# Strassen's scheme on twelve instead of eight chunks per block, with the half chunk, the folds and two layer-0 products laid out anew

## The chip, the core and the metric

The kernel runs on one core of a Trainium2 chip. The metric is the device time of one execution in microseconds (us). The engines are called PE (TensorE, matrix products), DVE (VectorE, elementwise work), ACT (ScalarE), POOL (GpSimd, which here only issues transfers that add) and SP (SyncE, which issues the loads).

## The reference

Three layers of a compressed interaction network. For each of 2048 batch items, with x of 39 fields by 16 channels and `prev` = x at first:

```python
for i, f in enumerate(CIN_LAYERS):              # f = 128 in each of the three layers
    h = prev.shape[1]                           # 39, then 64, then 64
    Wr = Ws[i].reshape(h, M, f)                 # M = 39
    z = relu(einsum('bhk,bmk,hmf->bfk', prev, x0, Wr) + bs[i][None, :, None])
    results.append(z[:, :64]); prev = z[:, 64:]
pooled = jnp.sum(jnp.concatenate(results, axis=1), axis=-1)
y = pooled @ W_lin
```

Everything is float32.

## The kernel before

**Blocks.** A block is 64 batch items by 16 channels, so 1024 columns (`NB`), treated as two halves of 512 (`BANK`, one bank of PSUM). There are 32 blocks. Blocks 0, 1, 30 and 31 are written out; blocks 2 to 29 run in a loop of 14 turns with two blocks each, an even one (`u` = 0) and an odd one (`u` = 1). In each turn of the loop DVE, PE, ACT, POOL and SP run their own instruction streams and meet at semaphores.

**Products.** In layers 1 and 2 the sum over pairs (h, m) is cut into 20 chunks of 128 pairs. DVE multiplies rows of `prev` with rows of x that were loaded repeated over partitions (`x_bc`), L408 for two chunks at once (128x2048) and L414 for one (128x1024), into a ring `prod` of 8 slots; PE multiplies a slot with the chunk's weights. `prod_ready` tells PE that a chunk is there, `chunk_used` tells DVE that a slot is free. The last field makes a half chunk, called T1: 64 rows for each half of the columns (two instructions of 64x512 in layer 1, L412; one of 64x1024 in layer 2, L405, into `left2`). Layer 0 has 6 chunks of its own (L381), made for the block that follows, and a remainder of 28 rows (`product_left`, once in a turn). PE works with two column halves of its array side by side: matmuls of 64 output rows.

**Order on PE in a looped block:** layer 1, layer 0 of the next block (L722), layer 2 (L921, L928). Layer 1 has 20 positions. Positions 0 to 15 are done for both halves of the columns, then positions 16 to 19 for the first half (`half_full` then lets ACT start with it), then 16 to 19 for the second half.

**Strassen's scheme.** On the second half of the columns, four pairs of chunks in layer 1 (`PAIR_TILES`, two pairs for each of the two layouts `a` of `prev`) go through seven quarter products of 256 columns (L850) instead of eight. It needs sums on DVE: `diff` (L474) and `more` (L479), made after each group of four chunks. Part of the quarter products collects in `acc0`. ACT copies one part out (L1090), DVE combines the parts in five small additions (L507 to L514) and adds them to `acc1` (L517, `mix`). That last addition waits until PE has consumed position 15, and PE waits for it (`mix_added`) before the second halves of positions 16 to 19. One field of each pair of x tiles must have another added to it, which POOL does by a transfer with addition (`add_tile`, L671).

**Evacuation and channel sums.** ACT applies bias and relu and spreads the state over partitions (`evacuate1_by_half`, `evacuate0`): `prev_ready` lets DVE begin the next layer. The kept halves (`res01`, `res2`) are folded twice by transfers with addition (`fold`, L677 and L680) and then reduced on DVE over the rest (L537) and weighed into `pool` (L549, L563).

Of the kernel before, what the change touches and what calls it, by code (L numbers as in the profile page):

```python
# [14 lines left out]
def cin_kernel(nc, x, w0, w0_mirror, w1, w2, b0, b1, b2, w_lin, out, dims):  # L15
# [29 lines left out]
    RUN_OF = [n for n, (_, w) in enumerate(RUNS) for _ in range(w)]  # L45
    NR = len(RUNS)
# [15 lines left out]
    MIX = 5  # L62
    assert NH == 2 and 2 * CH % RING == 0 and NBLK % U == 0 and HALF == 2 * QUAD and M == QPT * T + 3
# [8 lines left out]
    BC_LOADS = [QPT] * len(XB_GROUPS) + [1, 2]  # L72
# [20 lines left out]
    assert sorted(ORDER_PAIRED) == list(range(CH)) and all(p % RING + FOUR <= RING for p in FOUR_AT)  # L93

    with ExitStack() as ctx:
# [24 lines left out]
        x_rep_s = sb("x_rep_s", [P, BANK])  # L120
# [17 lines left out]
        sum01 = sb("sum01", [P, BB])  # L138
        sum2 = sb("sum2", [P, BB])
        pool = sb("pool", [P, BATCH])  # L140
        left2 = sb("left2", [P, NB])
# [1086 lines left out]
```

## Time and profile before

| | |
|---|---|
| median of 3 runs | 1970.98 us (1970.87 to 1971.71) |
| the profiled execution | 1970.57 us, its span 1968.6 us |
| PE busy | 1962.8 us (100%) |
| DVE busy | 1912.1 us (97%) |
| ACT busy | 586.7 us (30%) |
| POOL busy | 154.5 us (8%) |
| moved by transfers | 327.45 MB, mean 166 GB/s |
| granted TensorE clock | 1.000 |

Busy is the time in which at least one instruction of the engine is under way. Matmuls overlap in the pipeline, so PE's share says that it had work, not how fast that work went. The idle time before an instruction is put down to what ended it last.

### The profile page before, as it was taken

What the parts mean: (1) busy time and instruction counts of PE and PEld (TensorE: products, weight loads), DVE (VectorE), ACT (ScalarE), POOL (GpSimd) and SP (SyncE); (2) the same over time, 40 slices, a digit from 0 to 9 for tenths busy, and PEclk for the clock granted to TensorE, in tenths of its full rate; (3) what the DMA queues carried; (4) which work ended last, traced back from release to release, by engine and by line L of the source; (5) the groups of instructions that cost most, each with busy time, mean ns of one, the idle gap of its engine ahead of it and who ended that gap; (6) DMA issues with size and microseconds to landing.
All of it is one profiled execution on the core that took longest, in us unless ns stands there. A gap on an engine that the chain in (4) does not pass through costs nothing.

```text
span 1968.6 us, 29931 instructions
## 1 busy us (share of the span) xinstructions
PE 1962.8 (100%) x10304; PEld 739.1 (38%) x10304; DVE 1912.1 (97%) x1445; ACT 586.7 (30%) x717; POOL 154.5 (8%) x186
## 2 busy tenths in 40 slices
PE   9999999999999999999999999999999999999999
PEld 3333343333333333333343333333333333333333
DVE  8989999999999999999999999999999999999988
ACT  2333223332133322333222332223332133322332
POOL 1001000010100100001000010010100100000000
DMA  7999988788977889778798777987778977789720
GB/s 179 189 194 186 188 174 169 162 171 175 191 165 158 175 167 199 168 154 175 159 207 169 154 173 162 195 183 157 168 159 183 192 160 166 164 175 197 149 43 1
DMA packets 122523, 327.45 MB, mean 166 GB/s; under 512 B 24529, under 2 KB 43370, under 8 KB 122501
## 3 DMA queue, kind: packets, MB, share of 16 engines
q1 hardware_dynamic: 97539, 303.05, 71.2%
q0 software_dynamic: 24192, 23.87, 7.8%
q10 hardware_dynamic: 770, 0.23, 0.1%
q8 instruction: 15, 0.25, 0.1%
q14 instruction: 7, 0.06, 0.0%
HBM read 303.11 MB, written 0.01 MB: 154 GB/s over the span
## 4 chain that ended last, share of the span: by engine, by line
PE 97%; DVE 2%; DMA 0%; issue 0%; ACT 0%; ACTq 0%; DVEq 0%
PE acc L845 37%; PE acc L722 23%; PE acc L921 20%; PE acc L850 11%; PE acc L910 2%; PE acc L714 2%; DVE prod L408 1%; PE acc L789 1%; PE acc L935 1%; PE acc L928 1%; DMA bias<-b 0%; DVE prod L414 0%; PE acc L729 0%; ACT prev L1043 0%; ACTq L1141 0%
## 5 line engine op out<-in xcount | busy, mean ns | idle before, releaser
L408 DVE TENSOR_TENSOR prod<-prev,x_bc 128x2048 f32<-128x2048 f32 x511 | 1139.7, 2283 | 11.1 <-PE acc L722 9.4
L845 PE MATMUL acc<-prod,w_sb 128*64 128x512 f32 x3360 | 748.4, 593 | 0.0
L921 PE MATMUL acc<-prod,w_sb 128*64 128x512 f32 x1064 | 462.4, 593 | 0.1
L845 PEld LDWEIGHTS acc<-prod,w_sb 128*64 128x64 f32 x3360 | 237.3, 137 | 442.4 <-issue 391.4
L928 PE MATMUL acc<-prod,w_sb 128*64 128x512 f32 x840 | 384.3, 593 | 0.0
L722 PE MATMUL acc<-x_rot,w_sb 128*64 128x512 f32 x1240 | 277.5, 593 | 0.0
L1090 ACT ACTIVATE diff<-acc 64x256 f32<-64x256 f32 x56 | 21.3, 380 | 735.3 <-PE acc L850 735.0
L921 PEld LDWEIGHTS acc<-prod,w_sb 128*64 128x64 f32 x1064 | 143.9, 137 | 248.3 <-issue 193.5
L414 DVE TENSOR_TENSOR prod<-prev,x_bc 128x1024 f32<-128x1024 f32 x193 | 230.0, 1218 | 1.5
L381 DVE TENSOR_TENSOR x_rot<-x_rot,x_rep 128x1024 f32<-128x1024 f32 (+1 forms) x186 | 214.5, 1222 | 1.3 <-issue 0.3
L1014 ACT ACTIVATE prev<-acc,bias 32x1024 f32<-32x1024 f32 x140 | 155.1, 1108 | 3.1 <-DVE prod L408 0.9
L722 PEld LDWEIGHTS acc<-x_rot,w_sb 128*64 128x64 f32 x1240 | 87.8, 137 | 179.9 <-issue 164.8
L1107 ACT ACTIVATE prev<-acc,bias 32x512 f32<-32x512 f32 x224 | 152.4, 680 | 3.2
L1005 ACT ACTIVATE prev<-acc,bias 64x1024 f32<-64x1024 f32 x68 | 75.5, 1111 | 250.3 <-PE acc L722 221.7
L850 PE MATMUL acc<-prod,w_sb 128*64 128x256 f32 x672 | 134.0, 379 | 0.0
L722 PE MATMUL acc<-prod,w_sb 128*64 128x512 f32 x600 | 130.1, 593 | 0.6 <-DVE prod L408 0.5
L1101 ACT ACTIVATE prev<-acc,bias 64x512 f32<-64x512 f32 x112 | 76.5, 683 | 171.7 <-PE acc L845 170.7
L928 PEld LDWEIGHTS acc<-prod,w_sb 128*64 128x64 f32 x840 | 113.5, 137 | 8.8
L850 PEld LDWEIGHTS acc<-prod,w_sb 128*64 128x64 f32 x672 | 62.8, 137 | 64.0 <-issue 64.0
L671 POOL DMA_DIRECT2D x_bc<-x_bc x56 | 48.8, 872 | 411.9 <-DMA x_bc<-x 315.5
L677 POOL DMA_DIRECT2D res<-res x42 | 36.5, 869 | 559.7 <-ACT res L1126 363.2
L722 PEld LDWEIGHTS acc<-prod,w_sb 128*64 128x64 f32 x600 | 44.2, 137 | 86.1 <-issue 82.4
(100 smaller groups left out, 1246.7 us busy)
## 6 DMA issues: line engine op xcount, KB each, us to landing
x_bc<-x SPq DMA_DIRECT2D x312, 256.0 KB, 15.5
x_bc<-x SPq DMA_DIRECT2D x156, 512.0 KB, 21.4
x_rot<-x SPq DMA_DIRECT2D x155, 312.0 KB
x_rot<-x SPq DMA_DIRECT2D x217, 156.0 KB
x_bc<-x SPq DMA_DIRECT2D x124, 128.0 KB, 11.0
x_rep<-x SPq DMA_DIRECT2D x62, 192.0 KB
x_bc<-x_bc POOLq DMA_DIRECT2D x56, 128.0 KB, 10.1
x_rot<-x SPq DMA_DIRECT2D x124, 44.0 KB
```

Of the source, the lines that this page charges most:

```text
L381: nc.vector.tensor_tensor(x_rot[0:rows, c, :], rot, x_rep[0:rows, :], ALU.mult).then_inc(prod0_ready, 1)
L408: mul = nc.vector.tensor_tensor(prod[:, s:s + w, :], twice, x_bc[:, u, t:t + w, :], ALU.mult)
L414: mul = nc.vector.tensor_tensor(prod[:, s, :], old[:], new, ALU.mult)
L722: mm = nc.tensor.matmul(acc[f, h, :], w[:, f], rhs[:, BANK * h:BANK * h + BANK], start=start, stop=stop)
L845: mm = nc.tensor.matmul(acc1[f, h, :], w[:, f], prod[:, s, BANK * h:BANK * h + BANK], start=False, stop=stop, skip_group_check=closed)
L850: return nc.tensor.matmul(acc, w, rhs, start=start, stop=stop, skip_group_check=True)
L921: nc.tensor.matmul(acc2[0:HALF, u, :], w, prod[:, s, 0:BANK], start=(pos == 1), stop=False)
L928: mm = nc.tensor.matmul(acc2[HALF:P, u, :], w, prod[:, s, BANK:NB], start=(pos == 1), stop=False)
L1005: op = nc.scalar.activation(dst[0][HALF * g:HALF * g + HALF, :], src, ACT.Relu, bias=bias[HALF:P, layer:layer + 1])
L1014: op = nc.scalar.activation(dst[1][QUAD * q:QUAD * q + QUAD, :], acc[h:h + QUAD, :, :].rearrange("p h n -> p (h n)"), ACT.Relu, bias=bias[ ...
L1101: op = nc.scalar.activation(prev[1][0][HALF * g:HALF * g + HALF, cols], acc1[HALF:P, h, :], ACT.Relu, bias=bias[HALF:P, 1:2])
L1107: op = nc.scalar.activation(prev[1][1][QUAD * q:QUAD * q + QUAD, cols], acc1[f:f + QUAD, h, :], ACT.Relu, bias=bias[f:f + QUAD, 1:2])
```

## The change

The change has five parts. (1) `PAIR_TILES` gets a third pair: six chunks instead of four stand together in `prod` for each `a` (`six_chunks`), `diff` grows from 128x512 to 128x768 and `more` from 128x1024 to 128x1536 elements, and the third pair's `diff` product is done as two matmuls of 128 columns. Now positions 0 to 16 are consumed whole (`BY_HALF` = 17) and 17 to 19 by halves. (2) T1 is one DVE instruction of 128x512 in both layers, from `prev_t1`, which ACT writes with two more activations of 64x512 (`spread_t1`), and `x_t1`, which is loaded at half the size; in layer 2 it comes fifth. (3) In layer 2 the ring has a ninth slot, which shares its memory with `more`; SP's loads for `product_left` wait until `more` has been used, since `x_rep_s` lies there too, and `product_left` moves into the even block's layer 2. (4) `res01` is folded four times and `res2` three times, the folds of both alternating on POOL's queue with the tile additions of the next block (`block_adds`); DVE no longer reduces in the loop, it only weighs the folded columns, after the fifth run of layer 2. (5) Two of the six layer-0 products come ahead of `mix`, whose first addition waits for the first of ACT's two copies only.

```diff
+    T1_AT = 4
+    RUNS2 = [*RUNS[1:T1_AT + 1], RUNS[0], *RUNS[T1_AT + 1:]]
+    RUN_OF2 = [next(n for n, (p, w) in enumerate(RUNS2) if p <= pos < p + w) for pos in range(CH)]
...
-    PAIR_TILES = [(1, 2), (3, 4)]
-    FOUR = 2 * len(PAIR_TILES)
-    FOUR_AT = 2, 10
-    ORDER_PAIRED = [CH - 1, 0, *range(1, 1 + FOUR), *range(1 + FOUR, T), *range(T + 2, T + 2 + FOUR), T, T + 1,
-                    *range(T + 2 + FOUR, CH - 1)]
-    RUNS_PAIRED = [(0, 1), (1, 1), *((p, 2) for p in range(2, 14, 2)), (14, 1), (15, 1), (16, 2), (18, 2)]
+    PAIR_TILES = [(1, 2), (3, 4), (5, 6)]
+    SIX = 2 * len(PAIR_TILES)
+    SIX_AT = 2, 10
+    ORDER_PAIRED = [CH - 1, 0, *range(1, 1 + SIX), *range(1 + SIX, T), *range(T + 2, T + 2 + SIX), T, T + 1,
+                    *range(T + 2 + SIX, CH - 1)]
+    RUNS_PAIRED = [(0, 1), (1, 1), *((p, 2) for p in range(2, 16, 2)), (16, 1), (17, 1), (18, 2)]
     RUN_OF_PAIRED = [n for n, (_, w) in enumerate(RUNS_PAIRED) for _ in range(w)]
-    BY_HALF = 16
+    BY_HALF = 17
     MIX = 5
+    RING2 = RING + 1
+    SLOT2 = [(pos - 2) % RING2 for pos in range(CH)]
...
-        x_bc = sb("x_bc", [P, U, T + 2, NB])
+        x_bc = sb("x_bc", [P, U, T + 1, NB])
+        x_t1 = sb("x_t1", [P, U, BANK])
         prev = [[sb(f"prev{l}{a}", [P, NB]) for a in range(2)] for l in (1, 2)]
-        prod = sb("prod", [P, RING, NB])
-
-        diff = sb("diff", [P, 2, QTR])
-        more = sb("more", [P, 2, 2, QTR])
-        mixed = diff
+        prev_t1 = sb("prev_t1", [P, BANK])
+        prod_all = sb("prod", [P, RING * NB + len(PAIR_TILES) * BANK])
+        prod = prod_all[:, 0:(RING + 1) * NB].rearrange("p (s n) -> p s n", n=NB)
+
+        diff = sb("diff", [P, len(PAIR_TILES), QTR])
+        more = prod_all[:, RING * NB:].rearrange("p (k n c) -> p k n c", n=2, c=QTR)
+        x_rep_s = more[:, len(PAIR_TILES) - 1, :, :].rearrange("p n c -> p (n c)")
+        sum01, sum2 = diff[:, 0, 0:BB], diff[:, 0, BB:2 * BB]
+        mixed = diff[:, 0:2, :]
...
+                        sp.wait_ge(more_used, i * 2 - 1)
+                        sp.sem_inc(pairs_asked, 1)
...
-                if layer == 2 and t == T1:
-                    k = slice(HALF * u, HALF * u + HALF)
-                    mul = nc.vector.tensor_tensor(left2[k, :], old[k, :], new[k, :], ALU.mult)
+                s = (phase + pos) % RING if slots is None else slots[pos]
+                old = prev[layer - 1][a]
+                if t == T1:
+                    to = left2[:, u, :] if layer == 2 else prod[:, s, 0:BANK]
+                    mul = nc.vector.tensor_tensor(to, prev_t1[:], x_t1[:, u, :], ALU.mult)
                 elif w == 2:
                     twice = old[:].rearrange("p (o n) -> p o n", o=1).to_broadcast([P, w, NB])
                     mul = nc.vector.tensor_tensor(prod[:, s:s + w, :], twice, x_bc[:, u, t:t + w, :], ALU.mult)
-                elif t == T1:
-                    for h in range(NH):
-                        k, cols = slice(HALF * h, HALF * h + HALF), slice(BANK * h, BANK * h + BANK)
-                        mul = nc.vector.tensor_tensor(prod[k, s, cols], old[k, cols], new[k, cols], ALU.mult)
                 else:
-                    mul = nc.vector.tensor_tensor(prod[:, s, :], old[:], new, ALU.mult)
+                    mul = nc.vector.tensor_tensor(prod[:, s, :], old[:], x_bc[:, u, t, :], ALU.mult)
...
+                    elif pos in (0, 1, 11):
+                        dve.wait_ge(prev_ready[1], i * 2 + (1 if pos == 1 else 2))
                     if pos > 0:
-                        dve.wait_ge(chunk_used, first + pos + w)
-                    product(2, n, u, phase, runs=runs)
+                        dve.wait_ge(chunk_used, first + (pos + w - (1 if slots is SLOT2 else 0)))
...
+            def weigh_folded01(i, a, folded):
+
+                dve.wait_ge(folded01, folded)
+                nc.vector.tensor_scalar(pool[:, bass.ds(i * BB, BB)], res01[a][:, 0:BB], wl_col[:, 0:1], None,
+                                        ALU.mult).then_inc(pooled01, 1)
...
                     products1_paired(i, u, j + u, j, i * (2 * CH))
+                    products0(i + 1, range(2))
                     mix(i, u)
-                    if u == U - 1:
-                        product_left(j * U + (1 + U))
-                    channel_sum2(i - 2, folded=i * 32 - 32)
-                    products0(i + 1)
-                    channel_sum01(i - 1, 1 - u, folded=i * 32 - 32)
-                    products2(i, u, i * (2 * CH) + CH)
+                    products0(i + 1, range(2, C0))
+                    products2(i, u, i * (2 * CH) + CH, range(5))
+                    weigh_folded01(i - 1, 1 - u, i * (16 * FOLDS01) - 16 * FOLDS01)
+                    weigh_folded2(i - 2, i * (16 * FOLDS2) - 16 * FOLDS2)
+                    if u == 0:
+                        products2(i, u, i * (2 * CH) + CH, range(5, TAIL_RUNS))
+                        product_left(i + (1 + U))
+                        products2(i, u, i * (2 * CH) + CH, range(TAIL_RUNS, NR))
+                    else:
+                        products2(i, u, i * (2 * CH) + CH, range(5, NR))
...
+            def block_adds(i, u, loaded=None):
+
+                done01, done2 = i * (16 * FOLDS01) - 32 * FOLDS01, i * (16 * FOLDS2) - 32 * FOLDS2
+                pool.wait_ge(res01_ready, i * 2 + 1)
+                pool.wait_ge(pooled01, i)
+                fold(res01[1 - u], NB, 0, folded01, done01)
+                fold(res01[1 - u], NB, 1, folded01, done01)
+                pool.wait_ge(res2_ready, i + 1)
+                fold(res2, BANK, 0, folded2, done2)
+                fold(res01[1 - u], NB, 2, folded01, done01)
+                fold(res2, BANK, 1, folded2, done2)
+                if loaded is not None:
+                    add_tile(1 - u, 0, loaded)
+                fold(res01[1 - u], NB, 3, folded01, done01)
+                fold(res2, BANK, 2, folded2, done2)
+                if loaded is not None:
+                    for n in range(1, len(PAIR_TILES)):
+                        add_tile(1 - u, n, loaded)
...
-                quarter(acc0[low, u, 0, q2], s6[1], diff[:, 1, :], stop=(a == 1))
-                quarter(acc0[up, u, 0, q2], s6[0], diff[:, 0, :], stop=(a == 1)).then_inc(more_used, 1)
+                quarter(acc0[low, u, 0, q2], s6[1], diff[:, 1, :])
+                quarter(acc0[up, u, 0, q2], s6[0], diff[:, 0, :])
+                half = QTR // 2
+                quarter(acc0[low, u, 0, BANK - QTR:BANK - half], s6[2], diff[:, 2, 0:half], stop=(a == 1))
+                quarter(acc0[up, u, 0, BANK - half:BANK], s6[2], diff[:, 2, half:QTR], stop=(a == 1)).then_inc(more_used, 1)
...
+            def spread_t1(h, acc, layer, u):
+                k = slice(HALF * (h ^ u), HALF * (h ^ u) + HALF)
+                return nc.scalar.activation(prev_t1[k, :], acc[HALF:P, h, :], ACT.Relu,
+                                            bias=bias[HALF:P, layer:layer + 1])
...
-                    for q in range(QPT):
-                        f = HALF + QUAD * ((q + 1) % 2)
-                        op = nc.scalar.activation(prev[1][1][QUAD * q:QUAD * q + QUAD, cols], acc1[f:f + QUAD, h, :],
-                                                  ACT.Relu, bias=bias[f:f + QUAD, 1:2])
-                op.then_inc(prev_ready[1], 1)
+                    spread_t1(h, acc1, 1, a)
+                spread_turned(prev[1], acc1, 1)```

DVE at the end of a looped block's layer 1. Before, the products of positions 18 and 19 are followed at once by `mix`:

```order
L495 REGISTER_ALU
L408 TENSOR_TENSOR prod<-prev,x_bc 128x2048
L506 REGISTER_ALU
L507 TENSOR_TENSOR diff<-acc,diff 64x256
L508 ISA
L509 TENSOR_TENSOR diff<-acc,diff 64x256
L510 REGISTER_ALU
L511 TENSOR_TENSOR diff<-acc,diff 64x256
L512 TENSOR_TENSOR diff<-acc,diff 64x256
```

DVE at the same place in the changed kernel (L424 is the product of two chunks, L395 a layer-0 product):

```order
L509 REGISTER_ALU
L424 TENSOR_TENSOR prod<-prev,x_bc 128x2048
L405 ISA
L409 REGISTER_ALU
L395 TENSOR_TENSOR x_rot<-x_rot,x_rep 128x1024 x2
L521 TENSOR_TENSOR diff<-acc,diff 64x256
L522 ISA
L524 TENSOR_TENSOR diff<-acc,diff 64x256
```

Two of the six layer-0 products have moved from behind `mix` to a place ahead of it.

DVE between layer 0 and layer 2 before, with the reduction of `res01`'s folded columns and T1 as the first product of layer 2:

```order
L381 TENSOR_TENSOR x_rot<-x_rot,x_rep 128x1024
L381 TENSOR_TENSOR x_rot<-x_rot,x_rep 117x1024
L537 TENSOR_REDUCE sum<-x_seed 128x64
L548 REGISTER_ALU
L549 ISA
L549 TENSOR_SCALAR pool<-sum,wl_col 128x64
L405 TENSOR_TENSOR left<-prev,x_bc 64x1024
L532 REGISTER_ALU
L414 TENSOR_TENSOR prod<-prev,x_bc 128x1024
```

The changed kernel's DVE in layer 2 of an even block, from the run of positions 6 and 7 on:

```order
L424 TENSOR_TENSOR prod<-prev,x_bc 128x2048
L421 TENSOR_TENSOR left<-prev_t,x_t 128x512
L564 ISA
L565 ISA
L565 TENSOR_SCALAR pool<-x_seed,wl_col 128x64
L570 ISA
L573 ISA
L573 SCALAR_TENSOR_TENSOR pool<-res,wl_col,pool 128x64
L545 REGISTER_ALU
L424 TENSOR_TENSOR prod<-prev,x_bc 128x2048
```

The reductions are gone, T1 has half the columns, and T1 and both weighings stand behind four runs of layer 2.

PE behind a group of Strassen pairs before:

```order
L870 REGISTER_ALU
L850 MATMUL acc<-more,w_sums 64x256
L850 MATMUL acc<-more,w_sb 64x256
L850 MATMUL acc<-more,w_sums 64x256
L850 MATMUL acc<-more,w_sb 64x256
L850 MATMUL acc<-diff,w_sums 64x256 x2
```

PE at the same place in the changed kernel:

```order
L909 REGISTER_ALU
L889 MATMUL acc<-more,w_sums 64x256
L889 MATMUL acc<-more,w_sb 64x256
L889 MATMUL acc<-more,w_sums 64x256
L889 MATMUL acc<-more,w_sb 64x256
L889 MATMUL acc<-more,w_sums 64x256
L889 MATMUL acc<-more,w_sb 64x256
L889 MATMUL acc<-diff,w_sums 64x256 x2
L889 MATMUL acc<-diff,w_sums 64x128 x2
```

One pair's `more` products and two matmuls of 128 columns are added; ahead of them the third pair has taken the place of two chunks that were done whole.

## Rows read from the trace of the kernel before

**Rows 1.** The page: shares of the chain that ended last, by engine.
```profile
PE 97%; DVE 2%; DMA 0%; issue 0%; ACT 0%; ACTq 0%; DVEq 0%
```

**Rows 2.** Waits: engine, line, waited for: us in total, times, longest us.
```profile
PEld acc L921 <- DVE prod L408: 34.0, 83, 1.0
...
PEld acc L845 <- DVE prod L408: 25.6, 69, 0.8
...
DVE acc L517 <- PE acc L845: 5.1, 14, 0.4
```

**Rows 3.** Windows: the blocks 15 (odd) and 16 (even), from 938.25 us on.
```profile
938.25:1000.14 61.89, 61.89 (x334) 23.60 (x336) 61.14 (x48) 17.80 (x22) 4.35 (x5) 1.00 0.82 172
1000.14:1059.74 59.60, 59.60 (x321) 22.98 (x313) 58.46 (x45) 19.07 (x24) 6.08 (x7) 1.00 0.82 174
```

**Rows 4.** Timeline of PE in block 16: start us, us, engine, line, operation.
```profile
1000.14 1.04 PE L714 MATMUL acc<-prod,w_sb 64*64 64x512 f32 x8
...
1022.22 0.60 PE L850 MATMUL acc<-diff,w_sums 128*64 128x256 f32 x4
1022.65 10.47 PE L845 MATMUL acc<-prod,w_sb 128*64 128x512 f32 x48
1032.95 0.60 PE L722 MATMUL acc<-x_rot,w_sb 128*64 128x512 f32 x2
```

**Rows 5.** Timeline of DVE, from block 16's addition to block 17's.
```profile
1026.31 0.70 DVE L517 TENSOR_TENSOR acc<-acc,diff 128x512 f32<-128x512 f32 x1 [0.38 <-PE acc L845]
1027.04 0.29 DVE L537 TENSOR_REDUCE sum<-res 128x64 f32<-128x128 f32 x1
1027.49 0.28 DVE L563 SCALAR_TENSOR_TENSOR pool<-sum,wl_col,pool 128x64 f32 x1 [0.17 <-DVE sum L537]
1027.85 6.90 DVE L381 TENSOR_TENSOR x_rot<-x_rot,x_rep 128x1024 f32<-128x1024 f32 x6
1034.67 0.60 DVE L537 TENSOR_REDUCE sum<-x_seed 128x64 f32<-128x256 f32 x1
...
1035.59 1.21 DVE L405 TENSOR_TENSOR left<-prev,x_bc 64x1024 f32<-64x1024 f32 x1
...
1057.74 1.38 DVE L412 TENSOR_TENSOR prod<-prev,x_bc 64x512 f32<-64x512 f32 x2
...
1086.63 0.70 DVE L517 TENSOR_TENSOR acc<-acc,diff 128x512 f32<-128x512 f32 x1
```

**Rows 6.** Groups of like instructions: busy us, mean ns of one.
```profile
L479 DVE TENSOR_TENSOR more<-prod,diff 128x1024 f32<-128x1024 f32 x56 | 68.6, 1225 | 1.9
...
L474 DVE TENSOR_TENSOR diff<-prod 128x512 f32<-128x512 f32 x56 | 38.7, 692 | 1.9
...
L850 PEld LDWEIGHTS acc<-more,w_sums 128*64 128x64 f32 x224 | 30.7, 137 | 16.2
...
L995 PE MATMUL acc<-res,wl_all 128*32 128x64 f32 x16 | 1.1, 218 | 0.0
```

**Rows 7.** Timeline of ACT in block 16.
```profile
1022.87 0.77 ACT L1090 ACTIVATE diff<-acc 64x256 f32<-64x256 f32 x2 [21.71 <-PE acc L850]
...
1033.90 1.38 ACT L1101 ACTIVATE prev<-acc,bias 64x512 f32<-64x512 f32 x2
```

**Rows 8.** Timeline of POOL: folds and tile additions that it issues.
```profile
880.30 0.87 POOL L677 DMA_DIRECT2D res<-res  x1 [18.74 <-ACT res L1126]
892.61 0.86 POOL L680 DMA_DIRECT2D res<-res  x1 [11.44 <-DMA res<-res]
...
956.42 0.86 POOL L671 DMA_DIRECT2D x_bc<-x_bc  x1 [12.87 <-DMA x_bc<-x]
961.40 0.86 POOL L671 DMA_DIRECT2D x_bc<-x_bc  x1 [4.12 <-DMA x_bc<-x]
```

**Rows 9.** Timeline of ACT and DVE in the last block.
```profile
1937.13 2.25 ACT L1117 ACTIVATE prev<-acc,bias 64x1024 f32<-64x1024 f32 x2 [33.94 <-PE acc L722]
...
1940.31 1.22 DVE L405 TENSOR_TENSOR left<-prev,x_bc 64x1024 f32<-64x1024 f32 x1
```

More of the change, by code:

```diff
@@ L92, in cin_kernel @@
     assert RUN_OF[TAIL] == TAIL_RUNS and all((CH + TAIL + p) % RING + w <= RING for p, w in RUNS_LAST)
-    assert sorted(ORDER_PAIRED) == list(range(CH)) and all(p % RING + FOUR <= RING for p in FOUR_AT)
+    assert sorted(ORDER_PAIRED) == list(range(CH)) and all(p % RING + SIX <= RING for p in SIX_AT)
     with ExitStack() as ctx:
@@ L516, in mix, with products2 @@
                 dve.wait_ge(chunk_used, i * (2 * CH) + (RING + BY_HALF))
-                nc.vector.tensor_tensor(acc1[:, 1, :], acc1[:, 1, :], mixed[:].rearrange("p n c -> p (n c)"),
+                nc.vector.tensor_tensor(acc1[:, 1, :], acc1[:, 1, :], mixed.rearrange("p n c -> p (n c)"),
                                         ALU.add).then_inc(mix_added, 1)
-            def products2(i, u, first, part=range(NR), last=False, phase=CH):
-                runs = RUNS_END if last else RUNS
+            def products2(i, u, first, part=range(NR), last=False, slots=SLOT2):
+                runs = RUNS_END if last else RUNS2
                 for n in part:
@@ L695, in _ @@
             nc.gpsimd.tensor_tensor(w2_diff[:], second, first, ALU.subtract).then_inc(w2_diff_ready, 1)
-            with pool.Fori(1, STEPS - 1) as j:
-                for u in range(U):
-                    i = j * U + u
-                    for n in range(len(PAIR_TILES)):
-                        add_tile(u, n, (j + u) * (16 * QPT))
-                    pool.wait_ge(res01_ready, i * 2 + 1)
-                    fold(res01[1 - u], NB, folded01, i * 32 - 64)
-                    pool.wait_ge(res2_ready, i + 1)
-                    fold(res2, BANK, folded2, i * 32 - 64)
+            def block_adds(i, u, loaded=None):
[15 more added lines that the diff above has]
+                        add_tile(1 - u, n, loaded)
@@ L706, in _, with split @@
+            for n in range(len(PAIR_TILES)):
+                add_tile(0, n, 16 * QPT)
+            with pool.Fori(1, STEPS - 2) as j:
+                for u in range(U):
+                    block_adds(j * U + u, u, j * (16 * QPT) + 16 * QPT)
+            block_adds(LAST - 3, 0, (STEPS - 1) * (16 * QPT))
+            block_adds(LAST - 2, 1)
         @block.tensor
         def _(pe):
-            def split(acc, w, rhs, start, stop):
+            def split(acc, w, s, u, start, stop):
                 for h in range(NH):
-                    k = slice(HALF * h, HALF * h + HALF)
+                    k = slice(HALF * (h ^ u), HALF * (h ^ u) + HALF)
@@ L887, in layer1_paired @@
                     c = ORDER_PAIRED[pos]
-                    if pos in FOUR_AT:
-                        four_chunks(i, u, FOUR_AT.index(pos), runs)
-                    elif not any(p < pos < p + FOUR for p in FOUR_AT):
+                    if pos in SIX_AT:
+                        six_chunks(i, u, SIX_AT.index(pos), runs)
+                    elif not any(p < pos < p + SIX for p in SIX_AT):
                         pe.wait_ge(prod_ready, runs + RUN_OF_PAIRED[pos] + 1)
@@ L902, in layer1_paired, with layer2 @@
                     layer0_left(range(U), ahead)
-            def layer2(i, u, runs, part=range(1, CH), opened=False, run_of=RUN_OF, phase=CH):
+            def layer2(i, u, runs, part=range(1, CH), opened=False, run_of=RUN_OF2, slots=SLOT2):
                 if part[0] == 1 and not opened:
@@ L954, in _ @@
             layer2(0, 0, NR)
[L955 removed]
+            layer1(1, 1, 2 * NR, ahead=PAIR0 + 1)
             layer0(0, PAIR0 + 2)
@@ L1006, in spread @@
                                               bias=bias[HALF:P, layer:layer + 1])
-                op.then_inc(prev_ready[layer], 1)
+                if layer == 1:
+                    op.then_inc(prev_ready[layer], 1)
+                if t1_free is not None:
+                    act.wait_ge(prod_ready, t1_free)
+                for h in range(NH):
+                    op = spread_t1(h, acc, layer, u)
+                if layer == 0:
+                    op.then_inc(prev_ready[layer], 1)
                 spread_turned(dst, acc, layer)
```

217 lines of the change are left out of this document (109 added, 108 removed).

## The prediction, made before the changed kernel was run

> **What bounds the kernel now.** I read the page first. The chain that ended last lies on PE for 97% [rows 1], and PE and DVE are both busy almost throughout, so neither name alone is an answer. Busy says little of PE, so I looked at its pace: 48 matmuls of 512 columns start within 1032.95 - 1022.65 = 10.30 us, 0.215 us each, and four of 256 columns take 1022.65 - 1022.22 = 0.43 us, 0.108 us each [rows 4]. Time goes with the columns; there is no fixed part to see and hardly a gap.
>
> The loop is very regular. One turn is 61.89 us for the odd and 59.60 us for the even block, 121.49 us; DVE is busy for 61.14 + 58.46 = 119.60 us of it [rows 3]. Its missing 1.9 us are mostly the short gaps between instructions that depend on each other. The only real wait on PE is at L517 in the even block, 0.38 us, once in each of the 14 turns [rows 2, 5]. PE in turn waits for products of DVE, often and for at most 1.0 us, and those are waits of weight loads, most of which the running matmuls cover [rows 2]. I let 0.15 us a turn of them reach the matmuls; that is a choice, since no row separates them.
>
> So the limit is a loop through both engines: from the even block's L517 DVE works without a real pause to the odd block's L517 (1086.63 - 1026.31 = 60.32 us [rows 5]), and from there PE works without one to the next even block. Shortening one engine alone gives nothing; both get work removed here, and DVE gets some added. The question is which of the two hand-overs is late afterwards.
>
> **PE, own work.** A Strassen pair saves one quarter product, two matmuls of 256 columns in one of two column halves: 0.215 us by [rows 4]. Two pairs more per block, four per turn: -0.86 us a turn. The two matmuls of 128 columns in `six_chunks` count as one quarter. Nothing before has that shape; matmuls of 64 columns take 1.1 us for 16 [rows 6], 0.07 us each, so 128 columns are between 0.054 (by columns) and 0.14 us (twice that). As two column halves work side by side I take the columns' share; the upper bound would add at most 4 x 0.17 = 0.7 us a turn.
>
> **The weight loads** are what speaks against finer cutting. The change has 20 matmuls, and so 20 weight loads, more per block: 8 behind each of the two groups, 4 in layer 2. A load is 137 ns long [rows 6]. The steady 0.215 us per matmul, each with a load of its own, and the unchanged pace at 256 columns [rows 4] say that they are covered. I take nothing.
> The Trainium skill, page "TensorE: Matmul & The Clock Gate", section "The mechanism", says that a weight load overlaps with running matmuls only where the row group differs. All these matmuls use all 128 rows. By its section "LDWEIGHTS (loading the stationary operand)" 64 columns load in 53 ns, which makes an estimate of 20 x 53 ns = 1.1 us per block, 30 us in 28 blocks, and 1993 us in place of the sum below. The trace does not bear it out: at 0.215 us per matmul there is no room for uncovered loads [rows 4].
>
> **DVE, own work**, between the even block's L517 and the odd one's, where it decides:
> - the two reductions and their gaps and weighings go: 1027.85 - 1027.04 = 0.81 us, and 1035.59 - 1034.67 = 0.92 us [rows 5];
> - T1 in layer 2, 1.21 us long [rows 5], becomes 128x512, 0.69 us by `diff`'s shape [rows 6]: -0.52 us. T1 in layer 1, two pieces in 1.38 us [rows 5], becomes one: -0.69 us;
> - `diff` and `more` grow by 256 and 512 elements. A layer-0 product costs 6.90 / 6 = 1.15 us for 1024 [rows 5] and `diff` 0.69 us for 512, `more` 1.225 us for 1024 [rows 6], so about 1.04 ns per element: 0.80 us for a group, +1.60 us for two;
> - the two weighings remain, 0.25 to 0.3 us each and a gap: +0.6 us (0.4 if their register work is covered);
> - `product_left` moves into this stretch from behind the odd L517. It has `diff`'s old shape, 0.69 us, of which independent instructions overlap some 0.08 (1.21 long, 1.15 apart is the same effect): +0.6 us.
>
> Sum: 60.32 - 0.81 - 0.92 - 0.52 - 0.69 + 1.60 + 0.6 + 0.6 = 60.2 us. Over a whole turn DVE loses work: -1.73 x 2 - 1.21 x 2 + 3.2 + 1.2 = -1.5 us.
>
> **ACT.** The copies of L1090 start 0.04 us behind the `diff` matmuls' end and take 0.77 us for two [rows 7]; as the first addition now needs one only, `mix` starts 0.38 us earlier against PE. For layer 2 DVE needs PE's last second half, 0.17 us of pipeline, and then 1.38 us of two activations (as at 1033.90 [rows 7]). Before, the four turned copies of the first half came in between; now one T1 copy does, and ACT is ready in time. PE's second halves end at 29.81 + 2.58 = 32.4 us from the block's start (below), so the state is ready at 34.0; DVE gets there at 28.4 + 0.73 + 4 x 1.15 = 33.7. It waits 0.3 us where it waited for nothing: the stretch becomes 60.5 us. The extra T1 activations (4 x 0.68 us per block) lie in ACT's 70% idle time.
>
> **The hand-overs.** Times from a block's start on PE (1000.14 before [rows 4]). Position 14 begins at 22.5 and 16 at 25.94 before; with two pairs more, 16 begins at 25.5. It takes 8 x 0.215 = 1.72, the first halves of 17 to 19 take 2.58, so the second halves begin at 29.8 and layer 0 at 32.4 (32.81 before [rows 4], less 0.43).
> Even block: `more_used` comes at 25.7 with the pipeline's 0.17, the first copy ends at 26.1; DVE is there already, so it idles. The five additions take 2.3 us, L517 starts at 28.4 and ends at 29.1. PE needs it at 29.8: in time by 0.7 us.
> Odd block: DVE arrives 60.5 us later, at 88.9, ends L517 at 89.6 and PE hears of it at 89.65. PE's second halves could begin at (59.60 - 0.43) + 29.8 = 89.0. **PE waits 0.6 us, where it did not wait before.** This is the two-ahead order's price: the two layer-0 products fill DVE's idle time in the even block and delay `mix` by 2.3 us in the odd one. Cover before was 4 first halves, 3.4 us; now it is 3, 2.6 us. With DVE's figures 0.2 us lower the wait is 0.4; I take 0.5 us (0 to 1.2).
> Layer 2 itself gets easier: DVE makes its first product 34.0 - 32.4 = 1.6 us behind PE's start of layer 0, before 1035.59 + 1.13 - 1032.95 = 3.8 us [rows 4, 5], so the 0.15 us of waits at its end go.
>
> **Sum.** A turn: -0.86 - 0.15 + 0.5 = -0.51 us; 14 turns: -7.1 us. Blocks 0, 1, 30, 31 have no Strassen; in the last block DVE runs without a pause from 1940.31 and T1 there is 0.52 us shorter, while ACT, from 1937.13, then needs 1.38 us for T1 before the 2.2 us of state [rows 9], 1940.8 us: in time. -0.5 us. Together -7.6 us on the profiled 1970.57 us, 1963.0 us. The median of the runs is 0.4 us above the profiled one: **1963.3 us**. About 0.2% (4 us) is what a measurement of this kernel can tell from no change.
>
> **The folds**, if they are covered, cost nothing; the cover is thin in one place. `res2` of an even turn is issued at 880.30, and the step behind it goes out at 892.61 once that has landed [rows 8]: 12.3 us a step while the bulk loads run. Three steps end at 917.2. DVE asks in block 14 (which began at 1000.14 - 121.49 = 878.65) at 28.4 + 5.6 + four runs (7 chunks of 1.1, 7.7) + T1 0.6 + the first weighing = 42.6 us, so at 921.3: 4 us of cover, less what the steps of `res01` and the tile additions take in the same queue. Two tile additions were issued 5.0 us apart in a busy stretch and neither waited for the other [rows 8], so they overlap at least partly. `res01`'s own four steps begin about 17 us before the block and have more room. Nothing else asks earlier: the tile additions are for the next block.
>
> **Rivals.**
> A. *Both hand-overs are in time* (DVE's stretch under 60 us: the weighings hidden, no wait for the state). Then only PE's work counts: 14 x (0.86 + 0.15) + 0.5 = 14.6 us, 1956 us. For it: DVE loses 1.5 us a turn. Against: the sum above has PE waiting. Chance 0.22.
> B. *The odd hand-over eats the gain*: a wait of 1.0 us or more (weighings with unhidden register work, `diff` or `more` dearer than by element, 128-column matmuls at their bound). 1967 to 1972 us. Chance 0.14.
> C. *A fold is late* (the other side). DVE stands at `weigh_folded2` in the even block, inside the stretch that decides, so each us late is a us per turn. It eats the whole gain from 0.5 us late on, so from a third step landing at 921.8; 3 us late gives 1963.3 + 42 = 2005 us. For it: one step more on one queue, with three transfers of others in between. Against: 4 us of cover, and the bulk loads thin out towards the end of it. Chance 0.11.
> D. *Weight loads show*, at half of 137 ns since two column halves share them: 20 x 0.069 x 28 = 38 us, 2001 us. The pace of [rows 4] speaks against it. Chance 0.03.
> The forecast itself, 1958 to 1967 us, has 0.50.
>
> **The numbers.** The range leaves out C, D and the edge of A and B: 1955 to 1970.5 us. Faster: forecast 0.48 and A 0.22, with a little of B: 0.73. Same: the rest of the forecast and most of B: 0.12. Slower: C, D and a rest of B: 0.15.
>
> **What would show it.** Right: a turn of 121.0 us; a wait on `mix` of about 0.5 us on PE in odd blocks only, in even ones DVE idle for over 1 us before `mix`; 0.3 us of DVE for the state in even blocks; `diff` at 0.96 and `more` at 1.76 us; no wait at the weighings. Wrong: DVE idle on a transfer at L565 or L573; the `diff` matmuls of 128 columns at more than 0.22 us for four; PE slower than 0.215 us per 512 columns.

## The result: 4.5 us slower, and the profile after

| | before | changed |
|---|---|---|
| median, 15 runs each | 1971.05 us | 1975.59 us (1974.96 to 1976.19) |
| ratio | | 1.0024 (1.0017 to 1.0031) |
| span of the profiled execution | 1968.6 us | 1973.1 us |
| one turn of the loop (odd + even) | 121.49 us | 121.87 us |

The prediction was 1963.3 us, from 1955 to 1970.5, and faster at 0.73. The kernel became slower.

The page of the changed kernel: busy time by engine, then the chain that ended last.

```profile
PE 1955.2 (99%) x10864; PEld 782.7 (40%) x10864; DVE 1887.7 (96%) x1357; ACT 640.0 (32%) x732; POOL 256.7 (13%) x298
...
PE 65%; DVE 19%; issue 15%; DVEq 1%; ACT 0%; ACTq 0%
```

Both engines have less to do than before (PE 1962.8 us, DVE 1912.1 us), and yet the span is longer. The chain, which lay on PE for 97% [rows 1], now changes over to DVE often. Where an engine's work shrinks and the time doesn't, the difference is waiting; so the waits come next.

The waits of the changed kernel: engine, line, waited for: us in total, times, longest.

```profile
DVE prod L424 <- PE acc L970: 37.7, 28, 1.9
...
PEld acc L884 <- DVE acc L532: 29.6, 28, 1.5
...
PEld acc L963 <- DVE prod L424: 24.0, 70, 0.7
...
PE acc L884 <- DVE acc L532: 8.9, 14, 0.6
...
PE acc L963 <- DVE prod L424: 3.6, 14, 0.3
```

The first row is new and large: DVE waits once per block at a product of two chunks, for a matmul of layer 2, 37.7 us in all. Before, the one idle time of DVE in the loop that was put down to PE was the 5.1 us ahead of `mix`'s last addition [rows 2]; that row is gone. The fourth and fifth rows are new as well: PE itself stands still for `mix_added` (L532) in one block of each turn, and for a product of layer 2 in one block of each turn. These are the times in which all of PE was idle; the stall that can be read from the starts of the matmuls is a little longer (below).

Windows over block 15 (odd) and 16 (even): length, then each engine's busy time with its count, granted clock, DMA share, GB/s.

```profile
940.58:1002.77 62.19, 61.55 (x354) 25.31 (x356) 59.81 (x43) 19.42 (x22) 7.84 (x9) 1.00 0.80 163
1002.77:1062.46 59.69, 59.43 (x341) 24.41 (x333) 58.45 (x44) 20.56 (x24) 9.61 (x11) 1.00 0.90 182
```

Before, PE's busy time was the whole of both blocks [rows 3]; now it lacks 0.64 us in the odd and 0.26 us in the even one. DVE has 118.27 us of work in 121.87 us, where it had 119.60 in 121.49: 3.6 us of gaps and waits for 1.9.

DVE's timeline, from block 16's `mix` (even) into block 17's layer 2 (odd).

```profile
1029.36 0.42 DVE L521 TENSOR_TENSOR diff<-acc,diff 64x256 f32<-64x256 f32 x1
...
1031.72 0.70 DVE L532 TENSOR_TENSOR acc<-acc,diff 128x512 f32<-128x512 f32 x1
1032.45 4.63 DVE L395 TENSOR_TENSOR x_rot<-x_rot,x_rep 128x1024 f32<-128x1024 f32 x4
1037.00 1.22 DVE L426 TENSOR_TENSOR prod<-prev,x_bc 128x1024 f32<-128x1024 f32 x1
1038.14 6.69 DVE L424 TENSOR_TENSOR prod<-prev,x_bc 128x2048 f32<-128x2048 f32 x3
1044.74 0.68 DVE L421 TENSOR_TENSOR left<-prev_t,x_t 128x512 f32<-128x512 f32 x1
1045.35 0.25 DVE L565 TENSOR_SCALAR pool<-x_seed,wl_col 128x64 f32 x1
1045.51 0.28 DVE L573 SCALAR_TENSOR_TENSOR pool<-res,wl_col,pool 128x64 f32 x1
1046.56 2.29 DVE L424 TENSOR_TENSOR prod<-prev,x_bc 128x2048 f32<-128x2048 f32 x1 [0.78 <-PE acc L970]
...
1092.39 0.70 DVE L532 TENSOR_TENSOR acc<-acc,diff 128x512 f32<-128x512 f32 x1
...
1108.38 2.29 DVE L424 TENSOR_TENSOR prod<-prev,x_bc 128x2048 f32<-128x2048 f32 x1 [1.93 <-PE acc L970]
```

The wait sits at the product behind the two weighings, which is the run of positions 8 and 9: 0.78 us in the even block, 1.93 us in the odd one, together 2.71 us a turn, 37.9 us in 14 turns, which is the first row of the waits (37.7 us). Nothing is idle ahead of L521 in the even block, where the prediction had DVE idle for over 1 us; nothing is idle at L426 either, where it had 0.3 us for the state.

PE's timeline at three places: the second halves of layer 1 in block 15, the matmuls of 128 columns in block 16, the end of layer 2 in block 16.

```profile
968.74 1.89 PE L884 MATMUL acc<-prod,w_sb 128*64 128x512 f32 x8
971.27 2.79 PE L884 MATMUL acc<-prod,w_sb 128*64 128x512 f32 x12 [0.64 <-DVE acc L532]
...
1027.66 0.82 PE L889 MATMUL acc<-diff,w_sums 128*64 128x256 f32 x8
1028.31 1.03 PE L884 MATMUL acc<-prod,w_sb 128*64 128x512 f32 x4
...
1060.59 0.64 PE L963 MATMUL acc<-prod,w_sb 128*64 128x512 f32 x1 [0.26 <-DVE prod L424]
```

In block 15, 8 matmuls at 0.215 us take 1.72 us, but the next starts 971.27 - 968.74 = 2.53 us later: a stall of 0.81 us for `mix`. In block 16, `diff`'s eight matmuls (four of 256 and four of 128 columns) take 1028.31 - 1027.66 = 0.65 us, which is 4 x 0.108 + 4 x 0.054. The last row is the end of the even block's layer 2, where DVE is late with a product.

### The profile page after: what moved, and what is told of

Its sections match the earlier page's. It is cut to its first block, busy times and chain, and to the rows that moved or that the text cites. A ratio compares the mean times of both kernels' runs of the same rounds, so it can differ in the third digit from the quotient of the medians.

```text
span 1973.1 us, 31427 instructions
## 1 busy us (share of the span) xinstructions
PE 1955.2 (99%) x10864; PEld 782.7 (40%) x10864; DVE 1887.7 (96%) x1357; ACT 640.0 (32%) x732; POOL 256.7 (13%) x298
## 4 chain that ended last, share of the span: by engine, by line
PE 65%; DVE 19%; issue 15%; DVEq 1%; ACT 0%; ACTq 0%
PE acc L763 23%; PE acc L884 18%; DVE prod L424 12%; PE acc L963 10%; PE acc L889 8%; DVE prod L426 3%; PE acc L952 2%; DVE diff L488 1%; DVE x_rot L395 1%; PE acc L830 1%; PE acc L755 1%; PE acc L977 1%; DVE acc L532 1%; DVE x_rot_s L391 0%; PE acc L970 0%
## 5 line engine op out<-in xcount | busy, mean ns | idle before, releaser
L424 DVE TENSOR_TENSOR prod<-prev,x_bc 128x2048 f32<-128x2048 f32 x511 | 1141.9, 2283 | 53.3 <-PE acc L970 37.7
L884 PE MATMUL acc<-prod,w_sb 128*64 128x512 f32 x2912 | 662.6, 594 | 8.9 <-DVE acc L532 8.9
L963 PE MATMUL acc<-prod,w_sb 128*64 128x512 f32 x1064 | 465.3, 593 | 3.6 <-DVE prod L424 3.6
L970 PE MATMUL acc<-prod,w_sb 128*64 128x512 f32 x728 | 345.8, 594 | 0.0
L884 PEld LDWEIGHTS acc<-prod,w_sb 128*64 128x64 f32 x2912 | 203.0, 137 | 356.4 <-issue 302.6
L1143 ACT ACTIVATE diff<-acc 64x256 f32<-64x256 f32 x56 | 21.3, 380 | 807.0 <-PE acc L889 806.3
L889 PE MATMUL acc<-prod,w_sb 128*64 128x256 f32 x1344 | 282.6, 379 | 0.0
L1067 ACT ACTIVATE prev<-acc,bias 32x1024 f32<-32x1024 f32 x252 | 279.1, 1107 | 3.6
L426 DVE TENSOR_TENSOR prod<-prev,x_bc 128x1024 f32<-128x1024 f32 x193 | 230.8, 1217 | 10.2 <-ACT prev L1051 10.2
L963 PEld LDWEIGHTS acc<-prod,w_sb 128*64 128x64 f32 x1064 | 142.8, 137 | 230.8 <-issue 180.6
L704 POOL DMA_DIRECT2D res<-res x140 | 124.8, 922 | 764.0 <-DMA res<-res 424.3
L395 DVE TENSOR_TENSOR x_rot<-x_rot,x_rep 128x1024 f32<-128x1024 f32 (+1 forms) x186 | 216.1, 1218 | 0.9
L889 PEld LDWEIGHTS acc<-prod,w_sb 128*64 128x64 f32 x1344 | 140.3, 137 | 96.0 <-issue 96.0
L889 PE MATMUL acc<-prod,w_sums 128*64 128x256 f32 x1008 | 173.2, 379 | 0.0
L695 POOL DMA_DIRECT2D x_bc<-x_bc x84 | 72.9, 868 | 526.1 <-DMA x_bc<-x 368.9
L763 PE MATMUL acc<-prod,w_sb 128*64 128x512 f32 x600 | 130.0, 593 | 0.9 <-DVE prod L424 0.9
L1154 ACT ACTIVATE prev<-acc,bias 64x512 f32<-64x512 f32 x112 | 76.5, 683 | 126.7 <-PE acc L884 126.0
L889 PEld LDWEIGHTS acc<-prod,w_sums 128*64 128x64 f32 x1008 | 94.3, 137 | 48.6
L970 PEld LDWEIGHTS acc<-prod,w_sb 128*64 128x64 f32 x728 | 97.2, 137 | 9.9
## 6 DMA issues: line engine op xcount, KB each, us to landing
x_t<-x SPq DMA_DIRECT2D x64, 128.0 KB, 10.9
```

Of the source, the lines that this page charges most:

```text
L395: nc.vector.tensor_tensor(x_rot[0:rows, c, :], rot, x_rep[0:rows, :], ALU.mult).then_inc(prod0_ready, 1)
L424: mul = nc.vector.tensor_tensor(prod[:, s:s + w, :], twice, x_bc[:, u, t:t + w, :], ALU.mult)
L426: mul = nc.vector.tensor_tensor(prod[:, s, :], old[:], x_bc[:, u, t, :], ALU.mult)
L704: pool.dma_start(res[:, 0:n], res[:, n:2 * n], accum_op=ALU.add).then_inc(folded, 16)
L763: mm = nc.tensor.matmul(acc[f, h, :], w[:, f], rhs[:, BANK * h:BANK * h + BANK], start=start, stop=stop)
L884: mm = nc.tensor.matmul(acc1[f, h, :], w[:, f], prod[:, s, BANK * h:BANK * h + BANK], start=False, stop=stop, skip_group_check=closed)
```

## The experiments

Each edit is one against the changed kernel. The first three tell the causes apart, the next two look for the version that keeps the gain, the last two price parts of the change. The kernel before had a median of 1970.89 us beside e1, e2, e4 and e5, and 1970.95 us beside the other three.

**The theory.** In layer 2, DVE waits ahead of positions 8 and 9 until `chunk_used` counts `first + pos + w - 1`, one more than all of layer 1. T1, the position 0, doesn't lie in the ring, so PE counts it together with position 1; the wait is thus for PE to finish layer 2's position 1. With nine slots (`SLOT2`), positions 8 and 9 are written to slots 6 and 7, which layer 1's positions 14 and 15 used last and which have long been free. In the kernel before, with eight slots, the wait for position 1 was needed: position 9 was written to the slot that position 1 had used. The ninth slot took the need away, and the wait stayed.

The trace of before shows that DVE already met this wait in odd blocks. Block 17, PE's last matmuls on position 1 and DVE's run of positions 8 and 9, before:

```profile
1104.73 0.59 PE L921 MATMUL acc<-prod,w_sb 128*64 128x512 f32 x1
...
1105.37 2.29 DVE L408 TENSOR_TENSOR prod<-prev,x_bc 128x2048 f32<-128x2048 f32 x1
```

The same place in the changed kernel, where the run is the last row of DVE's timeline above:

```profile
1107.73 0.59 PE L963 MATMUL acc<-prod,w_sb 128*64 128x512 f32 x1
```

Before, the run starts at 1105.37, 0.05 us behind the end of these matmuls (1104.73 + 0.59 = 1105.32). In the changed kernel, where DVE does wait, it starts at 1108.38, just as far behind the end of its matmuls. In the even block 16 it started 0.17 us behind before (1044.46 against 1043.70 + 0.59). So DVE came to this wait 0.12 us after it was over in even blocks and just as it ended in odd ones, and no idle time showed it.

The rival: the two layer-0 products ahead of `mix` delay it in the odd block, and that costs the time whatever layer 2 does.

**e1_relax: the wait of positions 8 and 9 asks for layer 1 only.**

```diff
-    dve.wait_ge(chunk_used, first + (pos + w - (1 if slots is SLOT2 else 0)))
+    dve.wait_ge(chunk_used, first + (pos + w - ((2 if pos == 8 else 1) if slots is SLOT2 else 0)))
```

> The changed kernel with one wait eased: in layer 2 the run of positions 8 and 9 writes slots 6 and 7, last used by layer 1's positions 14 and 15, but waits until PE has consumed layer 2's position 1. Here it waits for layer 1 only. Theory 1 (this needless wait gives the gain back: DVE idles 0.78 us there in even and 1.93 us in odd blocks, and the even one lies on the loop that sets the pace): both idles go, the turn falls from 121.87 to 120.9 to 121.2 us, the time to 1962 to 1966 us; some 0.4 us of PE's 0.8 us wait for the addition in odd blocks stays. Theory 2 (the two layer-0 products ahead of mix are what delays PE, the wait only takes idle time that DVE has anyway): the turn stays within 0.2 us of 121.87, 1973 to 1976 us. Theory 3 (PE's own work has not become shorter, because of the finer cutting): nothing under 1971 us.

Measured: 1962.1 us (1961.85 to 1962.45), ratio 0.9955 (0.9941 to 0.9968): one number in one wait is worth 13.5 us. Windows over block 15 and 16, then waits, then DVE's timeline in block 16.

```profile
935.03:996.81 61.78, 61.55 (x355) 25.38 (x356) 61.30 (x44) 19.43 (x22) 7.86 (x9) 1.00 0.83 166
996.81:1055.96 59.15, 59.15 (x340) 24.83 (x332) 56.99 (x43) 20.59 (x24) 9.63 (x11) 1.00 0.89 181
```

```profile
DVE diff L521 <- ACT diff L1143: 19.5, 13, 1.5
PEld acc L884 <- DVE acc L532: 19.5, 28, 1.1
```

```profile
1022.98 0.42 DVE L521 TENSOR_TENSOR diff<-acc,diff 64x256 f32<-64x256 f32 x1 [1.50 <-ACT diff L1143]
...
1025.37 0.70 DVE L532 TENSOR_TENSOR acc<-acc,diff 128x512 f32<-128x512 f32 x1
...
1030.94 1.23 DVE L426 TENSOR_TENSOR prod<-prev,x_bc 128x1024 f32<-128x1024 f32 x1 [0.21 <-ACT prev L1154]
...
1039.65 2.28 DVE L424 TENSOR_TENSOR prod<-prev,x_bc 128x2048 f32<-128x2048 f32 x1
```

The wait at positions 8 and 9 is gone (1039.65 has none), PE has no wait left in the even block (busy for all of its 59.15 us), and DVE is early at `mix` by 1.50 us there. The turn is 120.93 us. What stays is a stall of 0.45 us for `mix` in the odd block (61.78 against 61.33 in e5 below), so the rival is true for that part, and only for that part.

**e2_behind: all six layer-0 products behind `mix` again.**

```diff
-                    products0(i + 1, range(2))
                     mix(i, u)
-                    products0(i + 1, range(2, C0))
+                    products0(i + 1)
```

> The changed kernel with all six layer-0 products behind mix, as before, and the wait of the run of positions 8 and 9 left alone. Theory 1: in even blocks mix has to wait for ACT's copy, so the layer-0 products that filled this time come 1.8 us later and layer 2 with them; PE then waits for its last products at the end of layer 2, about 2.2 us in place of 0.5; PE's wait in odd blocks (0.8 us) goes; together a turn of about 122.4 us, 1980 to 1985 us. Theory 2 (the two products ahead are the cause): the odd wait of 0.8 us goes and nothing takes its place, 121.1 us a turn, 1963 to 1966 us.

Measured: 1977.43 us (1977.04 to 1978.11), ratio 1.0034 (1.0022 to 1.0046). Windows over block 15 and 16, then two rows of the waits.

```profile
942.25:1003.59 61.34, 61.34 (x355) 25.38 (x357) 59.83 (x43) 19.41 (x22) 7.83 (x9) 1.00 0.79 166
1003.59:1064.28 60.69, 59.91 (x340) 24.10 (x332) 58.37 (x44) 20.57 (x24) 9.63 (x11) 1.00 0.85 177
```

```profile
DVE diff L521 <- ACT diff L1142: 39.4, 28, 1.9
...
PE acc L962 <- DVE prod L424: 10.9, 42, 0.3
```

The odd block is now without a stall, and the even one is 1.0 us longer. The rival wanted a turn of 121.1 us, and the run shows 122.03: it is out as the main cause. The theory had the direction right and too large a size (122.4 us, 1980 to 1985 us): it let DVE come to layer 2 in the even block 1.8 us later and left out that the 0.78 us of waiting at positions 8 and 9 go there. The run of positions 8 and 9 started 43.79 us into the even block in the changed kernel (1046.56 - 1002.77), and starts 44.81 us into it here, 1.02 us later:

```profile
1048.40 2.28 DVE L424 TENSOR_TENSOR prod<-prev,x_bc 128x2048 f32<-128x2048 f32 x1
```

DVE idles 39.4 us ahead of `mix`, 2.8 us a turn, with nothing to fill it, and PE pays for that in layer 2 (the second row: 10.9 us, 0.78 us in each turn, in which all of PE was idle; by the length of the even block it is 60.69 - 59.15 = 1.54 us).

**e3_relax_behind: both edits.**

> The eased wait of the first test, and all six layer-0 products behind mix in both blocks as in the second. Theory 1 in its plain form (the needless wait alone held the gain back) gives 120.5 to 121 us a turn, 1956 to 1964 us. By the walk through both queues it should give nothing: in the second test's even block the run of positions 8 and 9 started after position 1 had been consumed, so the eased wait was not felt there; DVE goes straight from ACT's copy to the end of layer 2, and PE waits there 1.5 us. So 122.0 us a turn, 1976 to 1978 us, the same as the second test: each of the two edits is worth something only with the other.

Measured: 1977.39 us (1977.3 to 1977.83), ratio 1.0035 (1.0021 to 1.0048). Window over block 16, then DVE's timeline there.

```profile
1003.90:1064.60 60.70, 59.92 (x340) 23.94 (x332) 58.16 (x44) 20.61 (x24) 9.63 (x11) 1.00 0.84 175
```

```profile
1030.07 0.42 DVE L521 TENSOR_TENSOR diff<-acc,diff 64x256 f32<-64x256 f32 x1 [2.09 <-ACT diff L1142]
```

A turn in the four combinations:

| | two products ahead of `mix` | all behind it |
|---|---|---|
| wait as changed | 121.87 | 122.03 |
| wait eased | 120.93 | 122.03 |

Alone, neither edit gives much: 0.16 us for the two products, nothing for the eased wait. Together they give 1.1 us. With all products behind `mix`, DVE's head start is lost there, in 2.1 us of idling in the even block. With the two ahead, it gets past `mix` and is lost at positions 8 and 9, unless that wait is eased too.

**e4_relax_even and e5_relax_one: fewer products ahead in the odd block.** e4 has the eased wait and puts two ahead in even blocks, none in odd ones. e5 puts one ahead in odd ones:

```diff
-                    products0(i + 1, range(2))
+                    ahead = 2 - u
+                    products0(i + 1, range(ahead))
                     mix(i, u)
-                    products0(i + 1, range(2, C0))
+                    products0(i + 1, range(ahead, C0))
```

> The eased wait, and two layer-0 products ahead of mix in even blocks only, none in odd ones. Theory 1 with what the first prediction says of the odd hand-over: DVE's addition in odd blocks comes 2.3 us earlier, PE waits for it no more, and layer 2 is still reached in time; only PE's own work is left, 120.5 us a turn, 1955 to 1959 us. Theory 3 (PE's own work is not shorter): about 121.3 us a turn, 1967 us or more. If DVE becomes late at the end of the odd block's layer 2 (its cover there is about 0.5 us by my sum), 120.6 to 121 us.

> The eased wait, two layer-0 products ahead of mix in even blocks and one in odd ones. The wait of PE that the first test leaves in odd blocks (0.4 us by my sum) is shorter than the 1.14 us by which the addition moves forward, so 120.5 us a turn as with none ahead in odd blocks, 1955 to 1959 us; if it is larger than with none ahead, the hand-over in odd blocks was later than I think.

Measured: e4 1956.07 us (1955.64 to 1957.65), ratio 0.9926 (0.9912 to 0.9939); e5 1955.71 us (1955.15 to 1956.58), ratio 0.9924 (0.991 to 0.9937). Windows of e5 over block 15 and 16.

```profile
931.89:993.22 61.33, 61.33 (x354) 25.46 (x356) 60.65 (x44) 19.40 (x22) 7.83 (x9) 1.00 0.83 168
993.22:1052.37 59.15, 59.15 (x340) 24.62 (x332) 57.54 (x43) 20.56 (x24) 9.60 (x11) 1.00 0.87 180
```

PE is busy for the whole of both blocks, 120.48 us a turn; this is its own work. e5 is 15.2 us below the kernel before and the best version here; e4 can't be told from it. The odd stall for `mix` is worth 1962.1 - 1955.7 = 6.4 us.

**f1_two_pairs: e5 with two Strassen pairs as before.** It takes back the third pair (`PAIR_TILES`, `RUNS_PAIRED`, `BY_HALF` = 16, no matmuls of 128 columns; `x_rep_s` gets memory of its own) and keeps all else.

```diff
-    PAIR_TILES = [(1, 2), (3, 4), (5, 6)]
+    PAIR_TILES = [(1, 2), (3, 4)]
...
-    BY_HALF = 17
+    BY_HALF = 16
```

> The fastest variant so far (eased wait, two products ahead of mix in even and one in odd blocks) with the third Strassen pair taken back: eight chunks as before, everything else of the change kept; x_rep_s gets memory of its own. If the third pair is worth what its columns say, PE's own work is 0.86 us a turn more and with all hand-overs in time the turn is 120.48 + 0.86 = 121.3 us, 1967 to 1969 us. If the finer cutting eats its own gain, the turn stays at 120.5, 1956 us. DVE has 3.2 us less per turn here, so no hand-over can be late.

Measured: 1967.07 us (1966.46 to 1968.03), ratio 0.9981 (0.9972 to 0.999). Windows over block 15 and 16.

```profile
936.62:998.35 61.73, 61.73 (x335) 23.79 (x337) 59.78 (x44) 19.42 (x22) 6.96 (x8) 1.00 0.84 165
998.35:1057.90 59.55, 59.55 (x321) 23.14 (x313) 55.48 (x43) 20.57 (x24) 8.74 (x10) 1.00 0.86 176
```

PE has no wait here either, so the two kernels differ by PE's own work: 121.28 against 120.48 us, 0.80 us a turn and 11.4 us in all; the faster one, e5, has 20 matmuls and 20 weight loads more per block. The remaining 3.9 us, by which f1 lies below the kernel before, are not taken apart by a run: about 3 us of them lie in the loop (121.28 against 121.49 us a turn), where PE has no wait now, and the rest outside it.

**f2_ring8: layer 2 in the ring of eight slots.**

```diff
-    SLOT2 = [(pos - 2) % RING2 for pos in range(CH)]
+    SLOT2 = [(CH + pos) % RING for pos in range(CH)]
...
-    dve.wait_ge(chunk_used, first + (pos + w - (1 if slots is SLOT2 else 0)))
+    dve.wait_ge(chunk_used, first + pos + w)
```

> The changed kernel (two ahead, wait not eased) with eight slots in layer 2 in place of nine. If the ninth slot brought nothing as the wait is written, because the run of positions 8 and 9 waits for position 1 with either ring and DVE lags behind PE from there on, the turn stays within 0.1 us of 121.87 and the time at 1975 to 1977 us. If the ninth slot was worth something in the changed kernel, the turn is longer, 1979 us or more.

Measured: 1975.36 us (1974.89 to 1976.16), ratio 1.0023 (1.0014 to 1.0033), a turn of 62.20 + 59.69 us. That is the changed kernel's time: as its wait was written, the ninth slot brought nothing.

## Why the prediction was wrong, by its own steps

**The step that failed** is in the hand-overs: "Layer 2 itself gets easier: DVE makes its first product [...] 1.6 us behind PE's start of layer 0, before [...] 3.8 us [...], so the 0.15 us of waits at its end go". The head start does come, but DVE can't keep it through layer 2. I asked when DVE can begin and summed its work from there; I didn't follow the count that each of its products waits for. In the odd block the four runs, T1 and the weighings now end before PE has finished layer 2's position 1, and DVE waits 1.93 us for it. From position 8 on its lead over PE (from the end of the product to PE's first matmul on it) is what it was: 2.64 us before and after in block 17, 2.53 before and 2.64 after in block 16; in e1 it is 4.65 and 3.60 us. The same count stood in the kernel before and cost nothing that its trace shows as idle time, since DVE came later: there T1 and a reduction stood ahead of layer 2's runs [rows 5]. But it came only as late as the wait let it in odd blocks, so that nothing of an earlier start could get past it.

The rest follows. In the even block `product_left` (0.6 us) stands behind the wait, so that DVE ends layer 2 late: PE waits 0.53 us there (59.68 on average over the turns, against the 59.15 of e5), where I had taken 0.15 us of waits away. In the odd block the lead at position 8 is the same 2.64 us, `product_left` is not there, and PE has no wait in layer 2; so it takes this product, on top of the short lead, to make the 0.53 us; in e1, with a lead of 3.60 us, it costs nothing. The two weighings stand ahead of the wait and cost nothing. The odd `mix` comes 0.95 us later than in e1, counted from the even block's start: 0.39 because the even `mix` does (28.95 us into the block in place of 28.56, as the 1.93 us lost in the odd block before have used up DVE's time in hand there), and 0.56 because of the 0.78 us in the even block, less the 0.21 us that e1 waits for the state. PE itself is 0.53 us late by then, so its wait for `mix` in the odd block grows from e1's 0.45 to 0.86 us (62.19 against 61.33), where I had 0.5. A turn is PE's own 120.48 + 0.86 + 0.53 = 121.87 us. I had 121.0. The difference, 0.89 us in each of 14 turns, is 12.5 us; the blocks outside the loop gave -0.6 us for the -0.5 I took.

e1 is nearly the kernel that I described: 1962.1 us for the 1963.3 predicted, a turn of 120.93 for 121.0. So I go through the other steps with it.

- *PE's own work*, -0.86 us a turn: right: f1 against e5 shows 0.80 (what makes the other 0.06 no run shows). The turn before, 121.49 us, is 1.01 above e5's, so the waits in it came to 0.15 to 0.21 us, for the 0.15 I chose.
- *Matmuls of 128 columns by columns*: right, eight in 0.65 us.
- *Weight loads covered* (rival D out): right. 20 more per block came with 0.80 us less a turn, not more. The Trainium skill, page "TensorE: Matmul & The Clock Gate", section "The mechanism", lets a weight load overlap only where the row group differs; by that rule f1, with 20 loads fewer per block over the same 128 rows, should have been the faster one, since the prediction's estimate of 1.1 us of loads per block is more than the 0.40 us that the pair saves. f1 is 11.4 us slower, so the trace does not agree with that rule; it fits the page's other condition in the same section, a load into the background weight buffer, though no run here shows into which buffer a load goes.
- *DVE's pieces*: `diff` 0.96 us and `more` 1.76, as the groups of the changed kernel show below. DVE's stretch from the even to the odd addition: 60.5 predicted, with 0.3 of waiting; 60.11 in e1 (1025.37 to 1085.48), with 0.21; in the changed kernel 1092.39 - 1031.72 = 60.67, of which 0.78 is the wait at positions 8 and 9. Without the waits it is 59.9 for 60.2: the two weighings take 0.36 us (1039.29 to 1039.65 in e1) where I had 0.6.
- *Even block*: right in e1. L521 was to start 26.1 us into the block, with DVE there before; it started at 1022.98 - 996.81 = 26.2, after 1.50 us of idling, and L532 at 28.6 for 28.4.
- *The two-ahead order's price*, PE waiting 0.5 us for `mix` in the odd block: right in e1 at 0.45, and e4 and e5 show it can be had back. It was 0.86 in the changed kernel for the reason above.
- *The folds* (rival C out): no row of the waits has DVE at L565 or L573. The last step for `res2` in block 16 is the last row below, issued at 1027.36; it landed at 1036.81, 8.7 us ahead of the weighing at 1045.51, for the 4 us I had.
- *Rival A*, both hand-overs in time, 1956 us: its time is that of e4 and e5 (1956.07 and 1955.71 us); it needed two more edits. *Rival B* had PE waiting longer for `mix` than 0.5 us, and it did, but 0.86 us and not the 1.0 or more that B asked for, and from none of the causes that B named.

Groups of like instructions of the changed kernel (busy us, mean ns of one), and POOL's timeline.

```profile
L493 DVE TENSOR_TENSOR prod<-prod,diff 128x1536 f32<-128x1536 f32 x56 | 98.4, 1758 | 1.9
...
L488 DVE TENSOR_TENSOR diff<-prod 128x768 f32<-128x768 f32 x56 | 53.7, 958 | 1.9
```

```profile
1027.36 0.89 POOL L704 DMA_DIRECT2D res<-res  x1 [4.22 <-DMA res<-res]
```

The rival that was missing is the one that came true: a head start that an old wait takes back. It was worth 0.95 us a turn by e1, 13.5 us in all. That e1 lies within 1.2 us of the 1963.3 says that the other terms held, not that the forecast did: it had not seen this wait at all.

Left open: what DVE would gain with `product_left` at another place. Moving that product by itself was not tried; its part in the even block's 0.53 us is read from the traces of the two blocks, not from a run without it.

## What to carry to other kernels

When an engine is let start earlier, walk every counted wait that it meets afterwards with the new times: a count that never showed as idle time can become the bound. The trace of before shows how much each has to spare, if the instruction's start is held against the end of what it waits for: here 0.12 us in the even block and nothing in the odd one. When a ring changes its size, or a thing outside it is counted with its neighbour, work out for each position who used its slot last, and wait for that and nothing later. A small loss in each of two engines can come from one wait far away; the first row of the waits that wasn't there before is where to look, and two edits that do nothing apart may need each other.

## What the runs showed of the hardware

Matmuls of 128 columns, each with a weight load of its own, still go by their columns in two column halves: 0.054 us each beside 0.108 for 256 and 0.215 for 512, with no fixed part to see. The loads' own length, 137 ns, is more than twice 0.054 us, and still nothing of it reached the matmuls in the 0.65 us of the eight. Only four such matmuls stand in a row here, between longer ones; a longer series of them no run shows.
